# Four layers of a graph network on one core: attribute sums in the rows of layer a, stored turned rows, fewer barriers

## What is computed

```python
h = maximum(layernorm(x), 0);  x = x + L0(h)     # layer a: attention, 1 head; batch norm; relu
h = maximum(layernorm(x), 0);  x = x + L1(h)     # layer b: attention, 4 heads, edge terms from 13 columns
h = maximum(layernorm(x), 0);  x = x + L2(h)     # layer c: edge MLP on [h, sum of 128 columns, u[batch]]
h = maximum(layernorm(x), 0);  x = x + L3(h)     # layer d: relational, 8 types
# L0: e = leaky_relu(a_src[src] + a_dst[dst]); alpha = softmax of e over the edges of a node and a self loop
#     out = segment_sum(alpha * (h @ W)[src], dst) + bias;  relu(batchnorm(out))
# L1: the same with 4 heads and an edge term; y = out + bias + h;  relu(layernorm(y) * gamma + beta)
# L2: agg = segment_sum(edge_attr_128, dst); relu(relu([h, agg, u] @ W1 + b1) @ W2 + b2) @ W3 + b3
# L3: relu(h @ W_self.T + b + segment_sum(((h @ W_rel[r])[src]), dst) / deg)
```

## The kernel before

| stage | from | to |
|---|---|---|
| graph: indices, layer a's table of rows | 0 | 316 |
| `expand_a`: destination logits spread over edges | 316 | 331 |
| sweep a: `attention_edges` for layer a, with the attribute sums, and the border crossings | 331 | 2397 |
| `nodes_a`: softmax joined with the self loop, batch norm, layer b's table | 2397 | 2731 |
| `expand_b` | 2731 | 2779 |
| sweep b | 2779 | 4820 |
| `nodes_b`: layer b joined, layer c's three products, layer d's table | 4820 | 5414 |
| `edges_rel`: sweep of layer d | 5414 | 7410 |
| `nodes_rel` | 7410 | 7553 |

## Time and profile before

### The profile page before, as it was taken

One profiled execution on the slowest core, in us unless ns is written; L12 is line 12 of the kernel. 1 busy time (PEld: TensorE's weight loads), 2 busy tenths in 40 slices (PEclk: granted clock), 3 DMA queues, 4 the chain that ended last, 5 costly groups with the idle time before them and its releaser, 6 DMA issues.

```text
span 7552.7 us, 21901 instructions
## 1 busy us (share of the span) xinstructions
PE 648.8 (9%) x2548; PEld 444.7 (6%) x2548; DVE 3346.4 (44%) x5068; ACT 1031.4 (14%) x3269; POOL 5330.3 (71%) x5506
## 2 busy tenths in 40 slices
PE   1100000000002410000000000137610000000000
...
GB/s 181 90 209 225 211 219 217 219 217 216 220 213 113 60 54 118 118 113 115 116 112 118 112 118 112 79 52 137 190 108 103 108 103 108 103 105 106 103 108 87
DMA packets 295746, 1022.73 MB, mean 135 GB/s; under 512 B 104343, under 2 KB 120855, under 8 KB 231975
## 3 DMA queue, kind: packets, MB, share of 16 engines
q1 hardware_dynamic: 114780, 644.98, 22.8%
...
...
HBM read 517.66 MB, written 503.28 MB: 135 GB/s over the span
## 4 chain that ended last, share of the span: by engine, by line
POOL 42%; issue 14%; PE 4%; DVE 3%; DMA 1%; POOLq 0%; ACT 0%; DVEq 0%; ACTq 0%; SPq 0%
POOL edge_rows L1025 20%; POOL edge_rows L1878 20%; POOL node_sums L1205 2%; PE ps L1775 2%; PE ps L1762 1%; DVE stats L1459 0%; PE ps L1816 0%; POOLq L165 0%; PE ps L1756 0%; DVE out_b L1297 0%; POOL attr_sums L1205 0%; PE ps L852 0%; DVE norm_mv L1463 0%; DVE dst_logit L672 0%; DVE node_sums L1288 0%
## 5 line engine op out<-in xcount | busy, mean ns | idle before, releaser
L1878 POOL DMA_INDIRECT edge_rows<-table_rel,rel_row x1568 | 1479.5, 944 | 604.0 <-issue 477.5
L1025 POOL DMA_INDIRECT edge_rows<-table_b,src_i x1568 | 1481.2, 945 | 513.0 <-issue 477.6
L1025 POOL DMA_INDIRECT edge_rows<-table_a,src_i x1568 | 1479.7, 944 | 485.6 <-issue 477.6
L1120 DVE TENSOR_TENSOR z<-edge_rows,dst_logit 128x16 f32<-128x16 f32 (+1 forms) x196 | 40.6, 207 | 1987.0 <-DMA edge_rows<-table_b,src_i 1169.9
L1938 DVE TENSOR_TENSOR edge_rows<-edge_rows,ps 128x2048 f32<-128x2048 f32 x97 | 221.9, 2288 | 1470.2 <-DMA edge_rows<-table_rel,rel_row 1470.2
L1092 ACT ACTIVATE edge_rows<-edge_rows,weight_decay 128x129 f32<-128x129 f32 x1552 | 465.4, 389 | 0.0
L1125 DVE TENSOR_TENSOR ps<-edge_rows,ps 128x2064 f32<-128x2064 f32 (+1 forms) x194 | 451.9, 2329 | 0.2 <-issue 0.2
L1159 DVE TENSOR_TENSOR edge_rows<-edge_rows,ps 128x2064 f32<-128x2064 f32 (+1 forms) x194 | 450.4, 2322 | 0.3 <-DVE edge_rows L1150 0.2
L858 PE MATMUL ps<-ident,edge_rows 128*1 128x128 f32 (+1 forms) x32 | 6.7, 398 | 4124.7 <-DVE edge_rows L1159 2078.3
L1083 ACT ACTIVATE ps<-weight_decay 128x128 f32<-128x128 f32 x97 | 27.3, 281 | 1899.4 <-DVE weight_decay L1163 1899.4
L1904 ACT ACTIVATE ps<-keep 128x16 f32<-128x16 f32 x97 | 19.5, 202 | 1904.8 <-DVE edge_rows L1938 1901.1
...
## 6 DMA issues: line engine op xcount, KB each, us to landing
...
edge_rows<-table_a,src_i POOLq DMA_INDIRECT x1568
edge_rows<-table_b,src_i POOLq DMA_INDIRECT x1568
```

Of the source, the lines that this page charges most:

```text
L1025: e.indirect_dma_start(out=rows[:, s, k, :], out_offset=None, in_=L.table, in_offset=bass.IndirectOffsetOnAxis(ap=src[:, at:at + 1], axis= ...
L1878: e.indirect_dma_start(out=rows[:, s, k, :], out_offset=None, in_=table_rel, in_offset=bass.IndirectOffsetOnAxis(ap=rel_row[:, at:at + 1], ...
```

## The change

1. **Attribute sums ride in layer a's rows.** The tile `edge_rows` of sweep a has rows of 258 floats, 130 for attention and 128 for attributes. The gathers write the first 130. SP loads the attributes into the other 128 (512 B per row), in 5 buffers with the rows in place of 4 of their own, and one store of 258-float rows replaces two. `sums_attr` is gone.
2. **The attribute crossing is woven into the softmax crossing** ("beside"): `Crossing` is split into t_turn, t_return, v_copy, v_scan and v_add, called between the steps of the other. Its 16 gathers are gone, since a head row now holds both.
3. **Turned and normed rows are stored for reuse.** In `nodes_a` the fetch brings 258 floats per node; PE transposes the attribute part, DVE and ACT copy it, SP stores it to `attr_turned`. POOL's fetch also waits for that. The relu(normed x) that `Table` makes is stored to `normed_b`. `nodes_b` loads both with SP instead of fetching, masking and transposing, and instead of ACT's recomputation.
4. **Layer b's bias is added in its table**, by a one-row matmul after each projection (the weights of a softmax sum to 1); POOL's addition (L1570) is gone.
5. **Zero row.** Each tensor of sums has one more row, of zeros; `sum_row` of a node without edges points to it, so the masks by `has` in the node stages are gone.
6. **Expand.** The first logit goes to a tile of its own, at once; there is no barrier between `expand` and its sweep, so POOL starts gathering while DVE spreads.

The diff, cut to its core:

```diff
-    A = Layer("a", 1, False)
+    A = Layer("a", 1, False, D)
     B = Layer("b", io["b_att_src"].shape[0], True)
-    sums_attr = dram("sums_attr", [EP + NV, D])
+    attr_turned = dram("attr_turned", [P, NK, JB * P])
+    normed_b = dram("normed_b", [NP, D])
...
+                at = ps[:, 2 + b // 3, (b % 3) * WX:(b % 3 + 1) * WX]
+                i = e.matmul(at, self.hT[:, k % 2, b * P:(b + 1) * P], self.weights.ext[:, :], start=True,
+                             stop=self.bias is None)
+                if self.bias is not None:
+                    i = e.matmul(at, ones[0:1, :], self.bias[:, :], start=False, stop=True)
...
+            for sums in (A.sums, B.sums, sums_rel):
+                width = sums.shape[1]
+                e.dma_start(sums[EP + NV:EP + NV + 1, :], zero[0:1, 0:width]).then_inc(zero_stored.sem, 16)
...
+            t = then(e.scalar_tensor_tensor(s2[:, :], s2[:, :], -float(EP + NV), s1[:, :], ALU.add, ALU.add))
+            e.wait_ge(*step.at(t))
+            t = then(e.tensor_tensor(s2[:, :], s2[:, :], has[:, :], ALU.mult))
+            e.wait_ge(*step.at(t))
+            t = then(e.tensor_scalar(s2[:, :], s2[:, :], float(EP + NV), None, ALU.add))
...
         def p_first(self, e):
+            e.indirect_dma_start(
+                out=self.at_first[:, :], out_offset=None, in_=self.L.node_logit,
+                in_offset=bass.IndirectOffsetOnAxis(ap=dst_first[:, 0:1], axis=0)).then_inc(self.first.sem, 16)
+
+        def v_spread(self, e):
             e.wait_ge(*self.loaded.at(16))
-            e.indirect_dma_start(
-                out=self.dst_l[:, 0, :], out_offset=None, in_=self.L.node_logit,
-                in_offset=bass.IndirectOffsetOnAxis(ap=dst_first[:, 0:1], axis=0)).then_inc(self.first.sem, 16)
-
-        def v_spread(self, e):
             e.wait_ge(*self.first.at(16))
+            e.tensor_copy(self.dst_l[:, 0, :], self.at_first[:, :]).then_inc(step.sem, 1)
+            step.up()
+            e.wait_ge(*step.at(step.n))
...
+        def scalar(e):
+            e.wait_ge(*terms_summed.at(B.H))
...
+            if self.beside:
+                e.wait_ge(*self.beside.added.at(1))
             e.dma_start(border_rows(self.L.sums), self.head[:, :, :]).then_inc(self.row_stored.sem, 16)
             e.wait_ge(*self.row_stored.at(16))
 
@@ -853,6 +869,8 @@
                                     start=True, stop=True)
                 return done
 
+            if self.beside:
+                self.beside.t_turn(e)
...
+            if self.beside:
+                e.wait_ge(*self.by_scalar.at(2))
+                self.beside.t_return(e)
...
-                        out=rows[:, s, k, :], out_offset=None, in_=L.table,
+                        out=rows[:, s, k, 0:L.W], out_offset=None, in_=L.table,
...
-                    if g >= NA:
-                        e.wait_ge(*attr_stored[g % NA].at(16 * (g // NA)))
-                        e.wait_ge(*attr_summed.at(g - NA + 1))
-                    e.dma_start(attrs[:, g % NA, :, :], attr[:, g, :, :]).then_inc(attr_loaded[g % NA].sem, 16)
+                    if g >= NS:
+                        e.wait_ge(*stored[g % NS].at(16 * (g // NS)))
+                        e.wait_ge(*attr_summed.at(g - NS + 1))
+                    e.dma_start(attrs[:, g % NS, :, :], attr[:, g, :, :]).then_inc(attr_loaded[g % NS].sem, 16)
...
-                e.dma_start(sum_rows(L.sums, g), rows[:, g % NS, :, :]).then_inc(stored[g % NS].sem, 16)
                 if attr is not None:
                     e.wait_ge(*attr_summed.at(max(g, 1)))
-                    e.dma_start(sum_rows(sums_attr, g), attrs[:, g % NA, :, :]).then_inc(attr_stored[g % NA].sem, 16)
-            if attr is not None:
-                crossing_attr.q_load(e)
+                e.dma_start(sum_rows(L.sums, g), rows[:, g % NS, :, :]).then_inc(stored[g % NS].sem, 16)
...
-            t2 = then(e.tensor_tensor(rm, rm, bc(has[:, j].unsqueeze(2), bj), ALU.mult))
...
+            for k in range(NK + 1):
+                if inside(k):
+                    nodes.q_own(e, k)
+                if inside(k - 1):
+                    e.wait_ge(*turned_av.at(k))
+                    e.wait_ge(*turned_as.at(k))
+                    e.dma_start(attr_turned[:, k - 1, :], attr_T[:, (k - 1) % 2, :]
+                                ).then_inc(turned_stored[(k - 1) % 2].sem, 16)
...
+                e.wait_ge(*table.normed.at(k + 1))
+                e.dma_start(normed_b.rearrange("(p j) d -> p j d", j=NJ)[:, span(k), :], table.hn[:, k % 2, :, :]
+                            ).then_inc(normed_stored[k % 2].sem, 16)
...
+                    e.wait_ge(*turn_a.at(k - 1))
                 nodes.p_fetch(e, k)
...
+            def turn_attr(k):
+                n = HALVES[0][1]
+                e.wait_ge(*turn_a.at(k + 1))
+                if k >= 2:
+                    e.wait_ge(*turned_stored[k % 2].at(16 * (k // 2)))
+                e.tensor_copy(attr_T[:, k % 2, 0:n * P], ps[:, 2, 0:n * P]).then_inc(turned_av.sem, 1)
...
+                if inside(i - 1):
+                    turn_attr(i - 1)
...
+                if inside(k):
+                    nodes.sums.wait(e, k)
+                    if k >= 1:
+                        e.wait_ge(*turned_av.at(k))
+                        e.wait_ge(*turned_as.at(k))
+                    for b in range(JB):
+                        i = e.transpose(ps[:, 2 + b // 4, (b % 4) * P:(b % 4 + 1) * P],
+                                        nodes.sums.buf[:, k % 2, b, A.W:A.WS], ident[:, :])
+                    i.then_inc(turn_a.sem, 1)
+                if inside(k - 1):
+                    e.wait_ge(*biased.at(k))
+                    i = column_sums(k - 1, chunk(agg, k - 1), 0)
...
+                if inside(i - 2):
+                    k = i - 2
+                    if k >= 2:
+                        e.wait_ge(*added_h1.at(k - 1))
+                    e.dma_start(h1[:, k % 2, :, :], normed_b.rearrange("(p j) d -> p j d", j=NJ)[:, span(k), :]
+                                ).then_inc(h1_loaded[k % 2].sem, 16)
+                if inside(i - 7):
+                    k = i - 7
+                    if k >= 2:
+                        e.wait_ge(*product_1.at(k - 1))
+                    e.dma_start(aT[:, k % 2, :], attr_turned[:, k, :]).then_inc(attr_loaded[k % 2].sem, 16)
...
         def gpsimd(e):
-            for i in range(NK + 8):
+            e.wait_ge(*bars_loaded.at(48))
+            for i in range(NK + 7):
                 if inside(i - 7):
                     k = i - 7
-                    attr.wait(e, k)
-                    at = attr.buf[:, k % 2, :, :]
-                    e.tensor_tensor(at, at, bc(has[:, span(k)].unsqueeze(2), [P, JB, D]), ALU.mult
-                                    ).then_inc(attr_masked.sem, 1)
                     e.wait_ge(*norm2.normed.at(k + 1))
-                    e.tensor_tensor(chunk(x, k), chunk(x, k), over_nodes(par[:, 3, :]), ALU.add
+                    e.tensor_tensor(chunk(x, k), chunk(x, k), over_nodes(par[:, 2, :]), ALU.add
                                     ).then_inc(x_biased.sem, 1)
-                if inside(i - 6):
-                    if i - 6 >= 2:
-                        e.wait_ge(*at_transposed.at(i - 7))
-                    attr.p_fetch(e, i - 6)
-                if inside(i - 2):
-                    k = i - 2
-                    if k == 0:
-                        e.wait_ge(*bars_loaded.at(64))
-                    e.wait_ge(*h1_normed.at(k + 1))
-                    at = h1[:, k % 2, :, :]
-                    e.tensor_tensor(at, at, over_nodes(par[:, 0, :]), ALU.add).then_inc(h1_biased.sem, 1)
                 if inside(i):
                     nodes.p_fetch(e, i)
...
-            def h1_norm(k):
-                if k >= 2:
-                    e.wait_ge(*added_h1.at(k - 1))
-                for b in range(JB):
-                    j = k * JB + b
-                    i = e.activation(h1[:, k % 2, b, :], x[:, j, :], ACT.Relu, bias=mean_nb[:, j:j + 1],
-                                     scale=mean_rs[:, j:j + 1])
-                i.then_inc(h1_normed.sem, 1)
...
-                    turn(i - 8, at_transposed, at_turned_v, aT, 0)
...
-                if inside(i - 8):
-                    k = i - 8
-                    e.wait_ge(*attr_masked.at(k + 1))
-                    free_low(i - 12, i - 9, i - 8)
-                    if k >= 1:
-                        e.wait_ge(*product_1.at(k))
-                    turn(0, attr.buf[:, k % 2, :, :]).then_inc(at_transposed.sem, 1)
...
             expand_a.sync(e)
+            edges_a.sync(e)
             finish_stage(e, 2)
-            edges_a.sync(e)
+            nodes_a.sync(e)
             finish_stage(e, 3)
-            nodes_a.sync(e)
+            expand_b.sync(e)
+            edges_b.sync(e)
             finish_stage(e, 4)
-            expand_b.sync(e)
+            nodes_b.sync(e)
```

349 lines of the change are left out of this document (172 added, 177 removed).

## The result

The changed kernel takes 7517.9 us (median of 5 runs, 7515.34 to 7520.53) against 7556.55 before; the ratio is 0.9949, 95% interval 0.9934 to 0.9963. So it is faster, but by 39 us in place of the 97 forecast, and outside the stated range. The profiled execution has a span of 7513.5 us; 39.2 us less than the one before.

| stretch | before | after | change | forecast |
|---|---|---|---|---|
| graph stage, to the load of the logits | 316.4 | 315.6 | -0.8 | 0 |
| spread and sweep of layer a, to DVE's last addition | 1996.1 | 1990.2 | -5.9 | -9 |
| crossing of layer a, to POOL's first fetch of nodes a | 85.1 | 75.9 | -9.2 | -8 |
| nodes of layer a | 334.0 | 409.8 | **+75.8** | **+13** |
| spread, sweep and crossing of layer b | 2089.2 | 2065.9 | -23.3 | -24 |

A forecast was written before the change was run, and what follows sets the result against it. POOL's gathers were taken to bound the sweeps, so gains lay only between them: -9 - 24 - 8 + 13 - 68 = -96 us, giving 7460 us; own range 7440 to 7480, wider range 7425 to 7505.

The forecast's parts named there:

- Nodes of layer a: +13: Node stage of layer a: longer fetch loop plus bias matmuls before the first chunk, 12 to 13 us slower.
- The fetch loop's own part: Nodes of layer a: turning attributes delays joining and POOL's next fetch, 0.5 us x 13 = 6.5, then 1.8 at the end.
- The +30 end: Nodes of layer a: upper end, if both DVE's wait and the bias matmuls count in every chunk.
- Spread of layer b: -24: Before sweep b: POOL gathers early, one gather per two-SBUF-input DVE instruction, 17 by the spread's end; 24.4 us earlier.
- Rival 1 (starvation): Spread of layer b: back-to-back DVE instructions let no gather through, gain only 10 us, time 7474; chance 14%.
- Spread of layer a -9 and its crossing -8: Layer a: gathering starts 12.9 us earlier, some 4 lost to DVE; separate attribute crossing of 17.6 goes, some 9.5 added elsewhere.
- Nodes of layer b: -68: Node stage of layer b: POOL loses gathers, masks and bias additions, DVE becomes the bound; -50, -14 and -4 us by steps.
- The holds as a sum: Nodes of layer b: DVE instructions held by POOL additions, about 39 us in all, of which 26 go.
- rival 2: Nodes of layer b: PE's chain or ACT takes over, DVE keeps its waits; -35 instead of -68, 7493; chance 10%.
- Sweep a: 0: Sweep of layer a: smaller load pieces raise the DMA share to 0.69, POOL stays the bound, no change.
- Rival 5: Sweep a: 512 B pieces make DMA the bound from 78 ns each; at 100 ns, 270 us more, 7730; chance 5%.
- the third: Nodes of layer a grow by 30 us instead of 13, time 7477; chance 7%.

The follow-up runs named there:

- the split product: Version with bias on DVE and decay row in PSUM, plus layer b's spread product split by head and DVE joining earlier in nodes a: 8189.53 against 8320.5 us, ratio 0.985.

## Why the prediction was wrong, point by point

- **Nodes of layer a: +13, measured +75.8.** The step that failed is the bias matmuls: "+3.7 before the first chunk is projected" and "The later chunks are covered by POOL's scatters ... against 7 to 8 us of the other engines (my estimate)". That estimate was not redone with the matmuls added. By the forecast's own figure, 0.27 us per record, a chunk is 28 x 0.27 + 1.9 + about 1 = 10.5 us of PE, over POOL's 8.9: at the lower clock the cover was gone by plain counting, for about 22 us. What the trace of before did not show is that 0.30 us come in at each change of the number of rows, 14 per chunk, and that the clock, which the table had reached before, would not rise: 14 x 0.48 + 14 x 0.30 + 1.75 + 0.78 = 13.4 us per chunk. The plain count alone does not cost the 22 us: with 128 rows and as many matmuls the clock rose, PE had slack, and the run was only 4.1 us slower than without a bias. So what failed is the cover, by the changes of rows and the clock that stayed low with them. The run without the bias takes 62.4 us off the stage, and that with 128 rows keeps all the rest of the change, so no other part of it has a share that shows. The fetch loop's own part was right: 8.3 forecast, 10.7 measured.
- **Ends of the range.** The +30 end of that term was said to be for bias matmuls that count in every chunk, but by the forecast's own 3.7 us per chunk these alone are 14 x 3.7 = 52; with the fetch loop's 8.3 the end should have been near +60, and the time near 7460 - 13 + 60 = 7507. A matmul of a shape that the trace did not show next to the others had no bound of its own.
- **Spread of layer b: -24, measured -23.3**, with the mechanism: one gather per DVE instruction with two SBUF inputs. The barrier put back cost 22.3, and PSUM operands brought 17.4 more. Rival 1 (starvation) did not come in the scans. It did in the split product, where one gather was held for 8.33 us over instructions of 2.9 us. The Trainium skill, "SBUF — State Buffer", section "A bandwidth-pool intuition that's wrong", has a DMA issued by GpSimd beside a DVE `tensor_copy` blocked until DVE's end plus about 115 ns. Here, beside scans and a product, the held gathers ended 0.74 to 0.81 us after DVE's end, as the one of the earlier trace rows did with 0.75; one takes 0.94 when nothing holds it.
- **Spread of layer a -9 and its crossing -8**: measured -5.9 and -9.2. Two gathers were held in the spread, 2.46 and 3.82 us; the sweep's last gather then began 8.4 us earlier (2278.64, before 2286.99), 0.8 of which the stage itself began earlier. DVE's work on the last group then began 6.0 us after that gather in place of 4.3, on the rows' landing: 8.4 - 0.8 - 1.7 = 5.9.
- **Nodes of layer b: -68, measured -76.1.** POOL's load was the cause, as said: 56 us came back with it. The holds as a sum were right, 25.3 us for 26, but not their places: L1297 had its 9, L1466 2 in place of 9, and L1479, not named, 8.5. The masks that DVE loses (6.1 us) were not in the sum. And the gathers cost through their place in POOL's queue (23 us in their run), where the forecast had them cost by filling POOL. That single terms were off and the sum near is in part luck. The "half clock" of rival 2 is a mean of 0.62 over both levels.
- **Sweep a: 0**, with the DMA share at 0.70. Rival 5 was far off: a piece took 26 ns, where it needed 78; the sum had 31.
- Of the rivals, only the third, nodes a at +30, had the place right, with less than half of the size. No rival named PE as the bound of that stage.
